# Last two mixes of a gated cross-attention and mixture-of-experts block: engine orders redone, batch 3's second shared block ahead of the expert loop, its down product in two parts behind it

## The reference, cut to what matters

```python
x = x + tanh(g_xattn) * einsum('bln,bmn->blm', layernorm(x), softmax(q @ k.T))   # q, k: 256 -> 128
flat = layernorm(x)                                     # 2048 tokens x 512
shared = (sigmoid(flat @ shared_gate.T) * (flat @ shared_up.T)) @ shared_down.T   # 352 wide
weights = softmax(flat @ router_w.T); top_w, top_idx = top_k(weights, 2)
he = sigmoid(xb @ wg[e]) * (xb @ wu[e]); de = he @ wd[e]                # bf16, 8 experts
x = x + tanh(g_ffn) * (flat + shared + sum over the two experts of top_w * de)
```

## Time and profile before

| | us |
|---|---|
| median of 3 runs | 347.29 |
| lowest, highest | 346.56, 349.27 |
| the profiled execution | 345.78 |
| its span | 344.0 |
| PE busy in the span | 300.4 (87%) |
| DVE, POOL, ACT busy | 216.7, 154.9, 133.1 |

### The profile page before, as it was taken

How to read it: one execution, slowest core, us unless ns; L and a number is a source line. 1 busy time by engine, 2 the same in 40 slices (tenths; PEclk the granted TensorE clock), 3 DMA queues, 4 the chain that set the end, 5 groups by cost and what they waited for, 6 DMA issues and landing times.

```text
span 344.0 us, 6138 instructions
## 1 busy us (share of the span) xinstructions
PE 300.4 (87%) x1594; PEld 213.3 (62%) x1608; DVE 216.7 (63%) x580; ACT 133.1 (39%) x236; POOL 154.9 (45%) x235
## 2 busy tenths in 40 slices
PE   8489789999999996199968948499999999999996
PEld 3357558777777675177856736366666666666764
DVE  1788776587655583455855486267777677674474
ACT  2272687416577427044403550033343333432100
POOL 3708891758304811900586045035565555556000
PEclk9999899999999999589989996699999999999999
DMA  7998896121410200000129998324344333457784
GB/s 240 355 213 287 135 205 241 52 73 61 174 73 2 92 31 0 0 2 2 46 77 169 208 207 212 79 77 124 97 118 117 99 100 115 122 145 242 233 328 183
DMA packets 30484, 45.90 MB, mean 133 GB/s; under 512 B 2880, under 2 KB 20032, under 8 KB 30464
## 3 DMA queue, kind: packets, MB, share of 16 engines
q1 hardware_dynamic: 19888, 27.66, 27.0%
q0 software_dynamic: 10432, 17.99, 22.2%
q10 hardware_dynamic: 144, 0.00, 0.0%
HBM read 39.58 MB, written 14.72 MB: 158 GB/s over the span
## 4 chain that ended last, share of the span: by engine, by line
PE 72%; DVE 9%; POOL 7%; issue 6%; DMA 3%; ACT 2%; SPq 0%; POOLq 0%; DVEq 0%; ACTq 0%
PE bank L769 14%; PE bank L505 12%; PE bank L506 11%; PE bank L507 11%; PE bank L786 7%; PE bank L500 4%; POOL xg L425 4%; PE bank L517 4%; PE bank L761 3%; PE bank L777 2%; POOL xT_lo L389 1%; DVE probT_lo L1146 1%; DMA xg<-lnb,slot 1%; DMA wqk_sb<-wqk 1%; DVE prob L1109 1%
## 5 line engine op out<-in xcount | busy, mean ns | idle before, releaser
L1041 ACT ACTIVATE sigc<-bank 128x352 f32<-128x352 f32 x39 | 18.1, 464 | 63.1 <-PE bank L769 63.1
L484 POOL DMA_INDIRECT z<-ysb,desti x36 | 36.0, 999 | 8.7 <-issue 8.4
L769 PE MATMUL bank<-wgu_lo,xTb 128*128 x156 | 36.7, 317 | 0.0
L769 PE MATMUL bank<-wgu_hi,xTb 128*128 x156 | 36.7, 317 | 0.0
L425 POOL DMA_INDIRECT xg<-lnb,slot x32 | 31.8, 994 | 10.2 <-issue 7.3
L1434 DVE TENSOR_TENSOR hrow<-sigc,bank 128x352 bf16<-128x352 f32 x39 | 20.3, 521 | 25.5 <-ACT sigc L1041 24.1
L1440 DVE TENSOR_SCALAR ysb<-bank,wt 128x512 bf16<-128x512 f32 x39 | 29.2, 748 | 4.9 <-PE bank L786 3.1
L505 PE MATMUL bank<-lnT_hi,sgu_lo 128*128 128x512 f32 (+2 forms) x72 | 30.1, 418 | 1.9 <-DVE lnT_lo L1146 1.9
L786 PE MATMUL bank<-wd_sb,hTb 128*128 (+1 forms) x106 | 29.4, 381 | 0.8 <-issue 0.2
L506 PE MATMUL bank<-lnT_lo,sgu_hi 128*128 128x512 f32 (+2 forms) x72 | 28.7, 399 | 0.0
L507 PE MATMUL bank<-lnT_hi,sgu_hi 128*128 128x512 f32 (+2 forms) x72 | 28.6, 398 | 0.0
(11 more groups left out here) (190 smaller groups left out, 698.2 us busy)
## 6 DMA issues: line engine op xcount, KB each, us to landing
xt<-xg SPq DMA_DIRECT2D x39, 129.0 KB, 2.2
xT_raw<-xT SPq DMA_DIRECT2D x4, 1024.0 KB, 7.2
acc<-x SPq DMA_DIRECT2D x4, 1024.0 KB, 9.4
out<-acc SPq DMA_DIRECT2D x16, 256.0 KB, 2.4
wgu_lo<-wguT POOLq DMA_DIRECT2D x2, 1408.0 KB, 13.3
wgu_hi<-wguT POOLq DMA_DIRECT2D x2, 1408.0 KB, 14.0
cx<-ctxT SPq DMA_DIRECT2D x4, 512.0 KB, 4.2
wd_sb<-wdT POOLq DMA_DIRECT2D x2, 1024.0 KB, 22.9
```

Source lines behind the costliest of these rows:

```text
L484: nc.gpsimd.indirect_dma_start(out=z, out_offset=bass.IndirectOffsetOnAxis(ap=desti[:, r:r + 1], axis=0), in_=ysb[:, r, :], in_offset=None ...
L769: mm = pe.matmul(bank[2 * v + half_][:, 0:I], xTb[:, v, k, :], wgu(k, bass.ds(e, 1), half_ * I, I), start=(k == 0), stop=(k == NT - 1))
```

## The change

POOL: batch 2's `factors2` and batch 3's `factor1` stand ahead of `x_low(3)`; the load of `wgu_hi` stands ahead of batch 2's scatters and waits for `tp` instead of `xmm`; `factors2(3)` stands between batch 2's two scatters, `wd_sb` behind the second. ACT: `x_high(3)` ahead of `normalise(3)`; `rows_again` behind `choice_exp`. PE: `turn_prob(3, 0)` and `(3, 1)` behind batch 1's down product, `mix(3)` ahead of `wide_shared(2, 1, 0)`, batch 3's block 1 (24 matmuls) ahead of the loop, and behind it the down product with its first two blocks ahead of most routed tiles. DVE follows. Banks, and where `sigc`, `ysb` and `hTb` lie, change so that this is free. `za(3)`, whose place `ysb` now takes, is loaded behind the loop.

Each tile's down product ends with one block instead of three, and two routed tiles come last. The diff, cut (left out: the places in memory, the waits of `turn_prob`, `turn_ln2`, `turn_logits` and `hidden_high` on the new banks, counts raised by one):

```diff
-    Z_BANK = [4, 5, 0, 1]
+    Z_BANK = [4, 5, 2, 3]
+    DOWN_BANK = [6, 7, 0, 1]
...
         def gate_bank(b, c):
-            return bank[0 if c == 1 or (b == last_b and c == 0) else 2]
+            if b == last_b:
+                return bank[0 if c == 0 else 2]
+            return bank[0 if c == 1 else 2]
...
         def logit_bank(b):
-            return bank[7 if b < last_b - 1 else 4]
+            return bank[{last_b: 4, last_b - 1: 1}.get(b, 7)]
 
         def rank_bank(b):
-            return bank[6 if b < last_b - 1 else 5]
+            return bank[{last_b: 5, last_b - 1: 0}.get(b, 6)]
...
-            for i in range(NB):
-                sp.dma_start(za[:, LT * i:LT * (i + 1)], zt[0, :, LT * i:LT * (i + 1)]).then_inc(s_za[i], 16)
+            def load_za(b):
+                sp.dma_start(za[:, LT * b:LT * (b + 1)], zt[0, :, LT * b:LT * (b + 1)]).then_inc(s_za[b], 16)
+
+            for b in range(last_b):
+                load_za(b)
             sp.wait_ge(s["cy"], NE)
             for r in range(SLOTS):
                 sp.wait_ge(s_yd[r], 16 * len(range(r, NE, SLOTS)))
             for i in range(0, TT, 2):
+                if i == LT:
+                    load_za(last_b)
                 sp.dma_start(zb[:, i:i + 2], zt[1, :, i:i + 2]).then_inc(s_zb[i // 2], 16)
-            for t in range(TT):
+            for t in [0, 1, 2, 3, 12, 4, 5, 13, 6, 7, 14, 8, 9, 15, 10, 11]:
                 if t < LT * last_b:
                     sp.wait_ge(s["comb"], t + 1)
...
             b = last_b - 1
-            x_low(last_b)
             factors2(b)
             factor1(last_b)
+            x_low(last_b)
             rows_copy(b)
-            scatter(b, 0)
-            scatter(b, 1)
-            factors2(last_b)
-
+            pool.wait_ge(s["xTlo"], NB)
             pool.wait_ge(s["eng"], TT)
-            pool.wait_ge(s["xmm"], TT)
+            pool.wait_ge(s["tp"], TT)
...
+            scatter(b, 0)
+            factors2(last_b)
+            scatter(b, 1)
+            pool.wait_ge(s["xmm"], TT)
             for k in range(IT):
...
             def wide_free(b, c, half_):
                 n = IT * b + c
-                if b == last_b and c:
-                    pe.wait_ge(s["ch"], NE)
+                if b == last_b and c == 2:
+                    pe.wait_ge(s["ch"], NE - 1)
+                elif b == last_b and c == 1:
+                    pe.wait_ge(*((s["sigd"], IT * b) if half_ == 0 else (s["hid"], IT * b)))
                 elif b == last_b:
                     pe.wait_ge(s["hid"], IT * (b - 1) + 2 - half_)
                 elif b == last_b - 1 and c == 2:
-                    pe.wait_ge(s["hid"], n)
+                    pe.wait_ge(s["hid"], n if half_ else n - 1)
+                elif b == last_b - 1 and c == 1:
+                    pe.wait_ge(s["place"], b + 1)
                 elif c == 0:
                     at_least(pe, s["hid"], IT * b)
                 elif c == 1:
-                    pe.wait_ge(s["expd"], TT if b >= last_b - 1 else LT * (b + 2))
+                    pe.wait_ge(s["expd"], LT * (b + 2))
                 else:
                     pe.wait_ge(s["hid"], IT * b + 1)
...
             def down(b, j, parts=range(IT)):
+                dst = down_bank(b, j)
...
+                if parts[0] == 0:
+                    if b == last_b:
+                        pe.wait_ge(*((s["yev"], NE) if j < 2 else (s["ch"], NE)))
+                    elif j >= 2:
+                        pe.wait_ge(s["shared"], LT * b + j - 1)
+                    else:
+                        pe.wait_ge(s["x1"], LT * (b + 1) + j + 3)
                 tok = slice(j * P, (j + 1) * P)
-                if b == last_b:
-                    t = LT * b + j
-                    pe.wait_ge(s_za[t // LT], 16)
-                    pe.wait_ge(s_zb[t // 2], 16)
-                    pe.matmul(bank[6 + j % 2][:, :], identb[:], za[:, t, :], start=True, stop=False)
-                    pe.matmul(bank[6 + j % 2][:, :], identb[:], zb[:, t, :], start=False, stop=False)
                 for c in parts:
                     pe.wait_ge(s["hlo"], IT * b + c + 1)
                     k = ORDER[c]
                     m = KI[k]
-                    mm = three(bank[6 + j % 2][:, :], hT_hi[0:m, k, tok], hT_lo[0:m, k, tok],
-                               sd_hi[0:m, k, :], sd_lo[0:m, k, :], c == 0 and b < last_b, c == IT - 1)
+                    mm = three(dst[:, :], hT_hi[0:m, k, tok], hT_lo[0:m, k, tok],
+                               sd_hi[0:m, k, :], sd_lo[0:m, k, :], c == 0, c == IT - 1 and b < last_b)
+                if parts[-1] == IT - 1 and b == last_b:
+                    t = LT * b + j
+                    pe.wait_ge(s_za[b], 16)
+                    pe.wait_ge(s_zb[t // 2], 16)
+                    pe.matmul(dst[:, :], identb[:], za[:, t, :], start=False, stop=False)
+                    mm = pe.matmul(dst[:, :], identb[:], zb[:, t, :], start=False, stop=True)
                 if parts[-1] == IT - 1:
                     mm.then_inc(s["dm"], 1)
...
             down(b - 1, 0)
-            turn_prob(last_b, 0)
-            turn_prob(last_b, 1)
             down(b - 1, 1)
             turn_ln2(b, 0)
             turn_ln2(b, 1)
@@ -724,15 +730,18 @@
             turn_ln2(b, 2)
             turn_ln2(b, 3)
             down(b - 1, 3)
+            turn_prob(last_b, 0)
+            turn_prob(last_b, 1)
             wide_shared(b, 0, 1)
             turn_prob(last_b, 2)
             turn_prob(last_b, 3)
             wide_shared(b, 0, 0, range(0, 2))
             turn_logits(b)
             wide_shared(b, 0, 0, range(2, NT))
+            mix(last_b, range(0, 1))
+            rank(b)
+            mix(last_b, range(1, LT))
             wide_shared(b, 1, 0)
-            rank(b)
...
             rank(last_b)
+            wide_shared(last_b, 1, 0)
+            wide_shared(last_b, 1, 1)
             for j in range(LT):
                 down(b, j)
...
-            wide_shared(last_b, 1, 0)
-            wide_shared(last_b, 1, 1)
             wide_shared(last_b, 2, 0)
-            pe.wait_ge(s["hid"], IT * last_b + 2)
-            for t in range(4):
-                routed(t)
             wide_shared(last_b, 2, 1)
-            for t in range(4, 8):
-                routed(t)
-            down(last_b, 0)
-            for t in range(8, 10):
-                routed(t)
-            down(last_b, 1)
-            for t in range(10, 12):
-                routed(t)
-            down(last_b, 2)
-            down(last_b, 3)
+            before_c2 = range(IT - 1)
+            only_c2 = range(IT - 1, IT)
+            down(last_b, 0, before_c2)
+            down(last_b, 1, before_c2)
+            down(last_b, 2, before_c2)
+            routed(0)
+            routed(1)
+            down(last_b, 3, before_c2)
+            pe.wait_ge(s["hid"], IT * NB)
+            routed(2)
+            routed(3)
+            down(last_b, 0, only_c2)
+            for j in range(1, LT):
+                for t in range(2 * j + 2, 2 * j + 4):
+                    routed(t)
+                down(last_b, j, only_c2)
+            routed(10)
+            routed(11)
...
             for j in range(LT):
                 soft(last_b, j)
+            x_high(last_b)
             for j in range(LT):
                 normalise(last_b, j)
+            for j in range(LT):
+                ln2_high(b, j)
             prob_high(last_b, 0)
             prob_high(last_b, 1)
-            x_high(last_b)
-            for j in range(LT):
-                ln2_high(b, j)
-            rows_again(b)
             logits_out(b)
             prob_high(last_b, 2)
             prob_high(last_b, 3)
             choice_exp(b)
+            rows_again(b)
             gate_shared(b, 0)
             for j in range(LT):
                 add_ln2(b, j)
             hidden_high(b, 0)
             gate_shared(b, 1)
-            ln2_high(last_b, 0)
-            ln2_high(last_b, 1)
+            for j in range(LT):
+                ln2_high(last_b, j)
             hidden_high(b, 1)
-            ln2_high(last_b, 2)
-            ln2_high(last_b, 3)
             gate_shared(b, 2)
-            rows_again(last_b)
             logits_out(last_b)
             act.activation(warm[:], less_mean[:], ACT.Exp)
+            rows_again(last_b)
+            choice_exp(last_b)
             hidden_high(b, 2)
-            choice_exp(last_b)
             gate_shared(last_b, 0)
             for j in range(LT):
                 add_ln2(last_b, j)
+            gate_shared(last_b, 1)
             hidden_high(last_b, 0)
+            hidden_high(last_b, 1)
...
-            for c in range(1, IT):
-                gate_shared(last_b, c)
-                hidden_high(last_b, c)
+            gate_shared(last_b, IT - 1)
+            hidden_high(last_b, IT - 1)
 
...
             over_sum(last_b, 3)
             residual(b, range(3, 4))
+            shared_out(b - 1, 0)
             ln2_apply(b)
+            ln2_low(b, 0)
+            ln2_low(b, 1)
```

(54 more changed lines are left out.)

53 lines of the change are left out of this document (20 added, 33 removed).

## The result

The changed kernel takes 323.56 us, the median of 4 runs (321.26 to 324.84), beside 346.93 for the kernel before (now also 4 runs, 346.17 to 349.27): a ratio of 0.9308, 95% interval 0.9231 to 0.9386. Single executions more than 1.5% above the fastest of the same kernel count as a slower state and are left out of medians and ratios; there were five, one each of e2_xlow_xhigh and e7_whole_down and three of the kernel before. The prediction was 323.6. The profiled execution took 324.84, its span is 323.1, the mean granted clock 0.974.

What follows compares the result with a forecast made beforehand. Before the loop a chain through POOL and DVE was taken to set the time, in and behind it PE. Gains of 18.5, 1.4 and 3.8 sum to 23.7 us: profile 322.1, median 323.6, range 319.5 to 331.

Steps and rivals of the forecast that it cites:

- Part 1: Batch 2's power ahead of `x_low(3)` on POOL: PE's 9.4 us idle becomes 1.1, half clock goes; gain 10.2 us.
- Part 2: Batch 3's norm: 18 matmuls instead of 6 cover the way to `turn_ln2(3, 0)`, power between scatters; gain 4.7 us.
- Parts 3 and 4: DVE order before `slot(3)`: low parts ahead of `sig`, gain 1.5 us; `hidden_low(2, 2)` and `weights` moved, gain 1.1.
- the count: Second estimate up to `rank(3)`, from counting PE's matmuls and transposes: 20.2 us gained, against 17.5 by summed terms.
- Part 5: Entry of the loop: batch 3's last scatter lands in 2.5 us instead of 3.88; gain 1.4, bounds 0 and -2.
- Part 6: Behind the loop: 24 fewer PE matmuls save 5.5 us, `zb` waiting costs 1.4 and DVE 0.3; gain 3.8 us.
- my second rival: Behind the loop, loads and stores fill the DMA engines and the end gives nothing: 327.4 us; chance 0.08.
- The clock: TensorE behind PE's new 1.1 us wait: a short gap costs nothing; like a long one, 1.9 us more.
- From the profile to the median: Whole kernel: the median of runs lies 1.5 us above the profiled execution, so 322.1 becomes 323.6.
- DVE and POOL in the second mix: Rival: late engines before batch 3's turn leave PE idle, half clock returns; 327 to 331 us, chance 0.12.
- `mix(3)` didn't wait: Rival: `mix(3)` waits for `x_low(3)` and the nine us come back; 333.8 us, chance 0.04.
- the loop's period: Rival: moved buffers lengthen each of 39 tiles, by 0.61 us losing all gain; 351 us at 0.75, chance 0.04.

Runs made afterwards that it cites:

- e2_xlow_xhigh: Changed kernel with `x_low(3)` ahead of batch 2's power on POOL and `x_high(3)` behind `normalise(3)` on ACT again; ratio 0.9576.
- e7_whole_down: Changed kernel with batch 3's down product left whole, all three blocks together behind block 2 and four routed tiles; median 326.85 us, ratio 0.9487.
- e8: Kernel before with one edit, on POOL: batch 2's power and factors and batch 3's `factor1` ahead of `x_low(3)`; 338.82 us, ratio 0.9755.
- e3: Changed kernel with batch 3's power (`factors2(3)`) behind both of batch 2's scatters instead of between them; 328.91 us, ratio 0.9484.
- e4: Changed kernel with two DVE orders undone: `shared_hidden(2, 1)` ahead of batch 3's `ln2_low`, `hidden_low(2, 2)` ahead of `weights` and `places`; 326.11 us, ratio 0.9377.
- e5: Changed kernel with the load of `wgu_hi` back behind batch 2's second scatter, just ahead of `wd_sb`'s; 334.05 us, ratio 0.9625.
- e6: Changed kernel with batch 3's block 1 (24 matmuls, its gate, hidden rows and low part) behind the loop again; 328.20 us, ratio 0.9449.
- e9: Changed kernel with SP's loads behind the loop in PE's order: `za(3)` ahead of the third `zb`, pairs reordered; 321.73 us, ratio 0.93.
- e12_again: The changed kernel run once more with no edit, in more rounds; 320.46 us, ratio 0.9265.

## Why the prediction was right

The forecast was 323.6, and 323.56 came out; of the difference to the kernel before, 23.7 were forecast and 23.8 to 24.2 measured from the zero on. Step by step:

- **Part 1** (10.2). The wait that was to be 1.1 is 0.77. `mix(3)` starts at 151.93, which is 18.0 behind the zero; by my sum it was 148.4, 17.8 behind it. Undoing it in one direction costs 8.2 (e2), doing it alone gives 9.3 to `slot` (e8): the mechanism is shown, the term a little large or shared with DVE's order.
- **Part 2** (4.7). No wait at `turn_ln2(3, 0)`. POOL was free 0.57 before it was needed; I had 0.6. e3 shows that the power's place carries it: 6.1. No run takes the 18 matmuls of cover away again, so their own share is open.
- **Parts 3 and 4** (2.6): 2.9 by e4.
- **Their sum**, 17.5 by the parts, 20.2 by the count, 18.5 taken: 19.0. The count is 1.2 off and the parts 1.5, too little to prefer either.
- **Part 5** (1.4): 1.5, and 2.49 to land where 2.5 was forecast. As a size this is right, as an account it is the weak step: "gain 1.4, bounds 0 and -2" looks at the load only where it stood. e5 shows that the early load is what allows the other parts. Without it, about 10.5 of the 19 us won before `slot` would have been lost again at the scatters' landing. My bounds for this step were taken from rows in which the scatters came 19 us later.
- **Loop** (0): 0.2 to 0.5.
- **Part 6** (3.8): 3.6 and 3.1. The 24 matmuls ahead of the loop are free there (e6), as said. But the account of its loss, "1.4 of waiting for `zb`", is half right: the wait is there, 1.05 and 1.66, and without it nothing is gained (e9), since loads and stores keep the DMA engines at 1.03 of their share. What ended the time was the mechanism of my second rival, to which I gave 0.08, not strong enough to take the 3.8, but level with PE.
- **The clock** (0). The new wait of 0.77 kept 1.00, as assumed, and that part of the forecast holds. But the way there, that a short gap costs nothing and a long one does, isn't what the runs show: a wait of 1.62 lost the clock at 46.95 in the changed kernel's own profile, and one of 3.90 kept it in e7_whole_down. That the short wait of part 1 was free is seen, and not explained by its length.
- **From the profile to the median** (+1.5). Put at the zero of before, the changed kernel's profile would have a span of 130.60 + 189.17 = 319.8 and, with the 1.7 around it, take 321.5, where my sum gave 322.1. Its early part was 3.3 late, and the median of its four runs lies 1.3 below it; that this ends within 0.1 of the forecast is luck. In the second series, 320.46 beside 345.91, the difference is 25.5 instead of 23.4.

The other rivals: DVE and POOL in the second mix came in time, by 0.57 us; `mix(3)` didn't wait, `xT_lo` being ready at 145.1 and wanted at 151.93; the loop's period didn't move with the addresses, 95.5 for 39 tiles against 95.7.

## What to carry to other kernels

When a chain is shortened, its last steps move towards transfers that used to be over by then: work out for every queue on the way what is still in it at the new time, not at the old. A short instruction that others wait for belongs ahead of a long one that nobody wants yet; that alone gave 8.8 of 24 us. And compare profiles from a common event behind the part that is the same in both, since that part can vary by more than a step of the change is worth.

## What the runs showed of the hardware

- The same first 128 us took between 128.65 and 133.93 to the zero over 14 profiles, a spread of 5.3 us, more than the 1% that a measurement of this kernel can tell. It goes with the clock. PE has up to four waits of over 1 us between 14 and 49 us. Sorted by how many of them the granted clock falls behind, the zero lies at 128.65 and 128.74 with none (e12_again, e7_whole_down), at 129.24 to 130.66 with one (seven profiles), at 132.41 to 133.82 with two (four), at 133.93 with three (the changed kernel's first).
- The length of a wait of PE doesn't tell alone whether the clock falls. It kept 1.00 behind waits of 1.54 (e4_sig_first, e8_before_one_edit), 2.04 (at 37.17 in e12_again) and 3.90 (e7_whole_down). It fell behind 1.62 at 46.95 in the changed kernel's first profile (0.52 in the 2 us behind), while the same wait at 43.03 in e12_again kept 1.00, and behind 1.86 in e6_block_behind (0.62). Behind each wait of 4.3 us or more in these profiles the 2 us that follow have 0.50. What the half clock then cost varied: 2.8 us after a wait of 4.68, 1.7 after 7.31 (e2_xlow_xhigh: `slot` 8.2 late, the first turn 6.5), 1.6 after 4.38. The longer wait was not the dearer one.
- A 0.19 us instruction of DVE took 1.52 beside POOL's 1.95 us cast. The kernel before has the like, `hT_lo` from two SBUF inputs at 184.63 with 1.95 instead of 0.69, beside POOL's cast from 184.09 to 186.03:

```profile
184.63 1.95 DVE L1286 TENSOR_TENSOR hT_lo<-sig,hT_hi 128x512 fp32r<-128x512 f32 x1
```
